# Last pair's scatters in portions, its tile list earlier, row loads bound to later additions

## The chip, the core and the metric

The kernel runs on 1 core of a Trainium2 chip. The metric is the time of one execution in device microseconds, a median of three runs. The engines are PE (TensorE), ACT (ScalarE), DVE (VectorE), POOL (GpSimd) and SP (SyncE, which here only issues transfers). Transfers issued by SP and POOL run on the same 16 DMA engines.

## What is computed

16 sequences of 512 tokens of width 128 go through two blocks. Cut to what matters (`_L0_attn_ref` is a Mamba-2 layer: input projection, convolution, scan, gated norm, output projection):

```python
h = _layernorm(x, axis=-1) * (1 + ca) + sa
x = x + ga * _L0_attn_ref(h, ...)
h = _layernorm(x, axis=-1) * (1 + cb) + sb
x = x + gb * _L0_ffn_ref(h, ...)
# _L0_ffn_ref: mixture of 8 experts, the two best of each token
gout = xt @ Wg.T
topv, topi = jax.lax.top_k(gout, K)
w = jax.nn.softmax(topv, axis=-1)
h = jax.nn.silu(g) * v          # g, v: two projections to 256 by the expert
eo = jnp.einsum('etf,ehf->eth', h, W3) + b3[:, None, :]
out = jnp.einsum('eth,te->th', eo, comb)
```

## The kernel before

The sequences are worked on in 8 pairs (`NP`), 1024 tokens each. For each pair the first block runs in chunks of 128 tokens; its result `x` is stored to `out` in HBM (`store_x1`). Then the router picks two experts for each token, and POOL *scatters* the tokens: 16 indirect transfers of 128 rows (`scatter(p, q)`, L419, two transfers a call, q from 0 to 7) write each token's row (`payload`: 128 values, the gate `gb`, the weight, the token number) to a place in the HBM buffer `rows` that belongs to its expert. q = 4 to 7 write the second choice and need the weights exchanged in `payload` first (`second_weight`, L430, which waits for the landing of the first 8 transfers).

The expert work is cut into 71 *tiles* (`NTILES`) of 256 rows of one expert. DVE writes the *list* of the tiles that have become full, pair by pair (`new_tiles`, L1082): the expert of a tile (`tile_e`) and its first row (`tile_row`). A tile t goes through:

- SP: `load_rows(t)` (L304, transfer at L318) brings 256 rows to `xs[t % 7]`; `load_weights(t)` (L294, transfer at L298) brings one expert's weights, 386 KB, to `wt[t % 4]`.
- PE: `expert_turn` (L1430) transposes the rows, `expert_up(t, 0)` and `(t, 1)` (L1438) make `FG` and `FV`, `expert_down` (L1448) the result in `FX`. ACT copies and takes silu (L652, L643), DVE multiplies (`expert_hidden`, L1120) and weights the result into `xs` (`expert_out`, L1130).
- POOL: `add_out(t)` (L436, transfers at L457) adds the 256 rows to `out` in HBM with two indirect transfers that accumulate.

Two executions of `add_out` that touch the same row must not overlap. The helper `landed(eng, t)` (L255) waits until the addition of tile t, and of all before it of its parity, has landed. `add_out(t)` always waits for `landed(t - 2)`; up to tile 49 it waits for `landed(t - 1)` too, and from tile 50 on only where the list says that the two may clash (`turn_of`, L448).

Tiles 0 to 48 come out of the first seven pairs' lists with a delay of 7 tiles (`LAG`). The last 22 tiles, 49 to 70 (`LAST`), come from the last pair's list. Their rows can be loaded once all 128 scatters have landed and the 8 *pads* have: SP writes 256 rows of zeros behind each expert's last row (`set_pads_of`, L300), called from `load_rows(49)`. `load_rows(t)` waits for the list, for the scatters of its pair, and for `landed(t - 7)`, since `xs` has 7 buffers.

All queues are written out by hand. On each engine a loop over i issues stage i's pieces of pairs i - 1, i, i + 1, i + 2 and of the tiles 8 i - 29 to 8 i - 14, in the written order; every engine works strictly in its order. In stage i = 8 the last pair's scatters are issued, each call between additions of the tiles 40 to 45. SP's order from tile 49 on, `r` for rows and `w` for weights: pads, r49, w49, r50, r51, r52, w50, r53, w51, w52, r54, w53, w54, r55, w55, r56, w56, r57, w57, r58, r59, r60, w58, r61, w59, w60, r62, w61, w62, r63, w63, r64, w64, r65, w65, r66, r67, r68, w66, r69, w67, w68, r70, w69, w70. PE's order in these stages is `expert_up(t, 0)`, `expert_down(t - 1)`, `expert_up(t, 1)`, with `expert_turn` one to three tiles ahead.

Of the kernel before, what the change touches and what calls it, by code (L numbers as in the profile page):

```python
# [30 lines left out]
NP = B // 2  # L31
# [4 lines left out]
PT = 2 * 2 * L // TR  # L36
LAG = E - 1
NTILES = NP * PT + LAG
# [3 lines left out]
DUMP = E * REGION + FIRST  # L42
XR = 3
WR, XSR = 4, 7
DOWN = 2 * FT * P
B12 = DOWN + FT * D
WT = B12 + 2 * FT
# [2 lines left out]
LAST = NTILES - (PT * (NP - 1) - LAG)  # L50
# [10 lines left out]
def program(nc, d):  # L61
    ctx = ExitStack()
    with ctx:  # L63
# [187 lines left out]
        def is_pair(p):  # L251
            return 0 <= p < NP

        def is_tile(t):
            return 0 <= t < NTILES  # L255

        def landed(eng, t):
            if t >= 0:
                eng.wait_ge(added[t % 2], 32 * (t // 2 + 1))
# [6 lines left out]
        @block.sync  # L266
        def _(sp_):
            xv = d["x"].rearrange("b (c p) m -> p b c m", p=P)
            ov = d["out"][0:NTOK, :].rearrange("(b c p) m -> p b c m", p=P, c=C)

            def load_x(p):
                sp_.dma_start(x[:, p % XR, :, :].rearrange("p (k c) m -> p k c m", k=2),
                              xv[:, 2 * p:2 * p + 2, :, :]).then_inc(x_in[p % XR], 16)

            def reload_x(p):
                if p >= XR:
                    sp_.wait_ge(x1_stored, 16 * (p - XR + 1))
                    sp_.wait_ge(xn2_ready, p - XR + 1)
                    load_x(p)

            def store_x1(p):
                sp_.wait_ge(x1_ready, p + 1)
                sp_.dma_start(ov[:, 2 * p:2 * p + 2, :, :],
                              x[:, p % XR, :, :].rearrange("p (k c) m -> p k c m", k=2)).then_inc(x1_stored, 16)

            def load_gates(p):
                wait(sp_, wo_ready, p - 1)
                sp_.dma_start(gate_a[:, p % 2, :, :],
                              d["gates"][2 * p:2 * p + 2, 0:D].partition_broadcast(P)).then_inc(gate_a_in[p % 2], 16)
                wait(sp_, payload_ready, p - 1)  # L290
                sp_.dma_start(gate_b[:, p % 2, :, :],
                              d["gates"][2 * p:2 * p + 2, D:2 * D].partition_broadcast(P)).then_inc(gate_b_in[p % 2], 16)

            def load_weights(t):  # L294
                sp_.wait_ge(seq_ready, pair_of_tile(t) + 1)
                wait(sp_, o_psum, t - WR + 1)
                e = sp_.value_load(tile_e[0:1, t:t + 1], min_val=0, max_val=E - 1)  # L297
                sp_.dma_start(wt[:, t % WR, :], d["wt"][bass.ds(e, 1), :, :].rearrange("o p n -> p (o n)")).then_inc(wt_in[t % WR], 16)  # L298

            def set_pads_of(e):  # L300
                r = sp_.value_load(pad_row[0:1, e:e + 1], min_val=0, max_val=DUMP)
                sp_.dma_start(d["rows"][bass.ds(r, TR), :].rearrange("(c p) m -> p c m", p=P), pad[:, :, :]).then_inc(pads_set, 16)

            def load_rows(t):  # L304
                p = pair_of_tile(t)
                sp_.wait_ge(seq_ready, p + 1)
                if t == 0:
                    sp_.wait_ge(dump_set, 32)
                if t == NTILES - LAST:
                    sp_.wait_ge(pads_ready, 1)  # L310
                    for e in range(E):
                        set_pads_of(e)
                if t >= NTILES - LAST:
                    sp_.wait_ge(pads_set, 16 * E)
                sp_.wait_ge(scattered, 16 * 2 * J * (p + 1))
                landed(sp_, t - XSR)
                r = sp_.value_load(tile_row[0:1, t:t + 1], min_val=0, max_val=DUMP + TR)  # L317
                sp_.dma_start(xs[:, t % XSR, :, :], d["rows"][bass.ds(r, TR), :].rearrange("(c p) m -> p c m", p=P)).then_inc(xs_in[t % XSR], 16)  # L318

            load_x(0)  # L320
            for dst, src in ((table[:, :], "table"), (wmod, "wmod"), (wout, "wout")):
                sp_.dma_start(dst, d[src]).then_inc(consts_in, 16)
            load_x(1)
            sp_.wait_ge(gate_step, 4)
            sp_.dma_start(d["gates"], gate_all).then_inc(gates_out, 16)
            load_x(2)
            sp_.dma_start(b3_rows, d["b3"]).then_inc(b3_in, 16)
            sp_.wait_ge(zero_ready, 1)
            sp_.wait_ge(pad_set, 1)
            sp_.dma_start(d["out"][NTOK:NTOK + 3 * TR, :].rearrange("(c p) m -> p c m", p=P),  # L330
                          zero[:, :].unsqueeze(1).to_broadcast([P, 6, D])).then_inc(dump_set, 16)
            sp_.dma_start(d["rows"][DUMP:DUMP + 2 * TR, :].rearrange("(c p) m -> p c m", p=P), dump_rows).then_inc(dump_set, 16)

            sp_.wait_ge(gates_out, 16)
            for i in range(-1, 13):
                if is_tile(PT * i - 27):
                    load_rows(PT * i - 27)
                if is_tile(PT * i - 29):
                    load_weights(PT * i - 29)
                if is_tile(PT * i - 28):  # L340
                    load_weights(PT * i - 28)
                if is_tile(PT * i - 26):
                    load_rows(PT * i - 26)
                if is_tile(PT * i - 27):
                    load_weights(PT * i - 27)
                if is_tile(PT * i - 26):
                    load_weights(PT * i - 26)
                if is_tile(PT * i - 25):
                    load_rows(PT * i - 25)
                    load_weights(PT * i - 25)  # L350
                if is_pair(i - 1):
                    store_x1(i - 1)
                if is_tile(PT * i - 24):
                    load_rows(PT * i - 24)
                    load_weights(PT * i - 24)
                if is_pair(i + 2):
                    reload_x(i + 2)
                if is_tile(PT * i - 23):
                    load_rows(PT * i - 23)
                    load_weights(PT * i - 23)  # L360
                if is_tile(PT * i - 22):
                    load_rows(PT * i - 22)
                if is_pair(i + 1):
                    load_gates(i + 1)
                if is_tile(PT * i - 21):
                    load_rows(PT * i - 21)
                if is_tile(PT * i - 20):
                    load_rows(PT * i - 20)
                if is_tile(PT * i - 22):
                    load_weights(PT * i - 22)  # L370
            sp_.wait_ge(x1_stored, 16 * NP)
            sp_.wait_ge(dump_set, 32)
            landed(sp_, NTILES - 2)
            landed(sp_, NTILES - 1)

        @block.gpsimd
        def _(pool):
# [58 lines left out]
            def add_out(t):  # L436
# [19 lines left out]
                for c in range(2):  # L456
                    pool.indirect_dma_start(d["out"], bass.IndirectOffsetOnAxis(ap=xs[:, t % XSR, c, PAY - 1:PAY].bitcast(U32), axis=0),  # L457
                                            xs[:, t % XSR, c, 0:D], None, compute_op=ALU.add).then_inc(added[t % 2], 16)

            for i in range(-2, 13):  # L460
                if is_pair(i - 2):
                    scatter(i - 2, 7)
                if is_tile(PT * i - 26):
                    add_out(PT * i - 26)
# [4 lines left out]
                    weight_by_decay(i, 2)  # L469
                if is_tile(PT * i - 25):  # L470
                    add_out(PT * i - 25)
                if is_tile(PT * i - 24):
                    add_out(PT * i - 24)
                if is_pair(i - 1):
# [314 lines left out]
        def _(vec):  # L789
# [340 lines left out]
            def expert_out(t):  # L1130
                vec.wait_ge(o_psum, t + 1)
                for c in range(2):
                    last = nc.vector.scalar_tensor_tensor(out=xs[:, t % XSR, c, 0:D], in0=FX[:, TR + c * D:TR + (c + 1) * D],  # L1133
                                                          scalar=xs[:, t % XSR, c, 2 * D:2 * D + 1], in1=xs[:, t % XSR, c, D:2 * D],
                                                          op0=ALU.mult, op1=ALU.mult)
                last.then_inc(ro_ready, 1)
# [7 lines left out]
            for i in range(-2, 12):  # L1144
# [33 lines left out]
                    softplus_rest(i + 1)  # L1178
                if is_tile(PT * i - 22):
                    expert_out(PT * i - 22)  # L1180
                if is_pair(i + 1):
                    conv_taps(i + 1, 4)
                if is_tile(PT * i - 21):
# [13 lines left out]
                    expert_out(PT * i - 20)  # L1197
                if is_pair(i):
                    mean_square(i)
                if is_pair(i - 1):  # L1200
                    new_tiles(i - 1)
                if is_pair(i):
                    residual(i)
# [38 lines left out]
        def _(pe):  # L1242
# [219 lines left out]
            for i in range(-2, 12):  # L1462
# [121 lines left out]
                if is_pair(i + 1):  # L1584
                    turn_y(i + 1, 0)
                    intra(i + 1, 1)
                if is_tile(PT * i - 15):
                    expert_turn(PT * i - 15)
                if is_pair(i):
                    turn_h2(i)  # L1590
                if is_tile(PT * i - 16):
                    expert_down(PT * i - 16)
                if is_pair(i + 1):
                    new_state(i + 1, 2)
                if is_tile(PT * i - 15):
# [71 lines left out]
```

## Time and profile before

| | us |
|---|---|
| median of 3 runs (823.67 to 825.77) | 825.5 |
| the profiled execution | 832.36 |
| span of its instructions | 830.5 |
| POOL busy, the whole span | 462.0 |
| mean busy share of the DMA engines, 640 to 706 us | 0.67 |
| the same, 729.3 to 822.7 us | 0.72 |
| PE busy, 729.3 to 822.7 us (93.4 us) | 65.9 |
| POOL busy, 729.3 to 822.7 us | 65.4 |

The page comes from one profiled execution; times inside the span count from its start. Busy time leaves out the issue of transfers by the sequencer. In a timeline row the first number is the start, the second the length, and the brackets hold the idle time before it with what ended it; a name as `out<-xs` is what is written and what is read. SPq and POOLq are the sequencers of SP and POOL.

### The profile page before, as it was taken

Reading aid. Unit: us, or ns where it says so; the run is one execution under the profiler, and the core shown is the slowest. Engines: PE = TensorE matmul, PEld = TensorE weight load, DVE = VectorE, ACT = ScalarE, POOL = GpSimd, SP = SyncE. Lnnn points to the kernel's source line nnn. Section 1 sums busy time; section 2 is a strip of 40 time slices with the busy share of each in tenths; the row PEclk is TensorE's granted clock in tenths of the full one; section 3 lists DMA queues with packets and bytes.
Section 4 is the critical chain, followed back from the end, with each engine's and each line's share of the span. In section 5 each row is a group of like instructions: output and inputs, shape, how many; then the busy total and the mean of one; then the engine's idle time right before and its main releaser. Section 6 shows DMA issues by size and latency. Waiting matters only on the chain. (4 is left out here: it accounts for less than half of the span.)

```text
span 830.5 us, 13734 instructions
## 1 busy us (share of the span) xinstructions
PE 680.6 (82%) x3713; PEld 518.9 (62%) x3713; DVE 559.4 (67%) x1640; ACT 516.8 (62%) x1223; POOL 462.0 (56%) x366
## 2 busy tenths in 40 slices
PE   3678899789789999998999999999966952774982
PEld 3246557556567776876787777768755731553662
DVE  2827967988986997898689978987743561231421
ACT  3784795896796899687969977886522310221320
POOL 2003004444453378757775786688687477357775
PEclk9779798999998999999999999999996967897997
DMA  5100001112013465455346444653645774857973
GB/s 186 28 0 1 1 27 32 45 52 71 33 58 102 119 168 129 105 155 125 92 105 174 107 97 103 204 104 90 180 107 120 200 204 95 202 123 149 191 169 28
DMA packets 81275, 88.86 MB, mean 107 GB/s; under 512 B 7360, under 2 KB 67696, under 8 KB 81200
## 3 DMA queue, kind: packets, MB, share of 16 engines
q1 hardware_dynamic: 54528, 61.37, 25.6%
q0 software_dynamic: 26672, 26.62, 18.0%
q8 instruction: 31, 0.51, 0.3%
q14 instruction: 44, 0.36, 0.2%
HBM read 54.50 MB, written 33.46 MB: 106 GB/s over the span
## 5 line engine op out<-in xcount | busy, mean ns | idle before, releaser
L457 POOL DMA_INDIRECT out<-xs x142 | 226.8, 1597 | 116.9 <-issue 53.2
L427 POOL DMA_INDIRECT rows<-payload,pos x128 | 131.6, 1028 | 68.2 <-issue 30.2
L880 DVE SCALAR_TENSOR_TENSOR xbc<-T,table,xbc 128x511 f32<-128x511 f32 (+2 forms) x192 | 141.9, 746 | 7.7 <-ACT xbc L599 3.1
L1133 DVE SCALAR_TENSOR_TENSOR xs<-FX,xs 128x128 f32<-128x128 f32 x142 | 43.1, 345 | 122.6 <-PE FX L1457 104.7
L1457 PE MATMUL FX<-wt,hid 128*128 128x128 f32 x568 | 87.8, 301 | 17.2 <-DVE hid L1125 17.2
L655 ACT ACTIVATE xt<-FX 128x256 f32<-128x256 f32 x71 | 27.0, 380 | 110.1 <-PE FX L1434 96.0
L1457 PEld LDWEIGHTS FX<-wt,hid 128*128 128x128 f32 x568 | 73.7, 203 | 26.6 <-DVE hid L1125 17.9
L648 ACT ACTIVATE sg<-FG,wt 128x256 f32<-128x256 f32 x142 | 59.3, 471 | 47.0 <-PE FG L1444 38.4
L1444 PE MATMUL FG<-xt,wt 128*128 128x256 f32 x284 | 77.6, 397 | 12.1 <-DMA wt<-in_wt 8.1
L1287 PE MATMUL T<-h,win 128*128 128x512 f32 x128 | 76.7, 698 | 12.4 <-DVE xbc L880 10.6
L1444 PE MATMUL FV<-xt,wt 128*128 128x256 f32 x284 | 78.2, 400 | 0.0
L630 ACT ACTIVATE mda<-table,da 128x128 f32<-128x128 f32 x256 | 77.7, 397 | 0.0
L1125 DVE SCALAR_TENSOR_TENSOR hid<-FV,wt,sg 128x256 f32<-128x256 f32 x142 | 62.0, 479 | 22.5 <-issue 13.3
L599 ACT ACTIVATE xbc<-T,table 128x512 f32<-128x512 f32 x64 | 49.5, 773 | 40.3 <-PE T L1287 35.8
L385 POOL TENSOR_TENSOR rstd<-var,table 128x8 f32<-128x8 f32 x16 | 26.6, 1663 | 78.4 <-DVE var L826 63.9
L1346 PEld LDWEIGHTS YA<-xdt,decay 128*128 128x128 f32 x512 | 66.9, 207 | 2.8 <-issue 1.7
L1346 PE MATMUL YA<-xdt,decay 128*128 128x64 f32 x512 | 66.6, 288 | 1.0 <-issue 1.0
L1444 PEld LDWEIGHTS FG<-xt,wt 128*128 128x128 f32 x284 | 52.4, 200 | 20.3 <-DMA wt<-in_wt 9.7
L406 POOL TENSOR_TENSOR xdt<-tok,dt 128x512 f32<-128x512 f32 x32 | 34.8, 1088 | 51.5 <-ACT tok L566 51.3
L527 ACT ACTIVATE xn<-x,shift,rstd 128x128 f32<-128x128 f32 x128 | 50.9, 484 | 17.5 <-DVE shift L844 16.4
L1444 PEld LDWEIGHTS FV<-xt,wt 128*128 128x128 f32 x284 | 52.4, 201 | 8.5 <-issue 3.8
L1434 PE MATMUL FX<-table,xs 128*128 128x128 f32 x142 | 29.3, 290 | 31.8 <-DMA xs<-rows 27.8
(207 smaller groups left out, 1343.5 us busy)
## 6 DMA issues: line engine op xcount, KB each, us to landing
wt<-in_wt SPq DMA_DIRECT2D x71, 386.0 KB
xs<-rows SPq DMA_DIRECT2D x71, 258.0 KB
x<-in_x SPq DMA_DIRECT2D x8, 512.0 KB, 4.3
out<-x SPq DMA_DIRECT2D x8, 512.0 KB
out<-xs POOLq DMA_INDIRECT x142
rows<-pad SPq DMA_DIRECT2D x8, 258.0 KB
rows<-payload,pos POOLq DMA_INDIRECT x128
gate_a<-gates SPq DMA_DIRECT2D x8, 128.0 KB, 4.3
```

Source lines behind the costliest of these rows:

```text
L427: pool.indirect_dma_start(d["rows"], bass.IndirectOffsetOnAxis(ap=pos[:, k, n:n + 1], axis=0), payload[:, n, :], None).then_inc(scattered, 16)
L457: pool.indirect_dma_start(d["out"], bass.IndirectOffsetOnAxis(ap=xs[:, t % XSR, c, PAY - 1:PAY].bitcast(U32), axis=0), xs[:, t % XSR, c, 0 ...
L527: last = nc.scalar.activation(dst[:, j, :], src[:, j, :], ACT.Identity, bias=shift[:, j:j + 1], scale=rstd[:, j:j + 1])
L599: nc.scalar.activation(xbc[:, t, k, :], T[:, k, :], ACT.Identity, bias=conv_b[:, t:t + 1], scale=conv_w[:, t * KC + KC - 1:t * KC + KC]).t ...
L630: last = nc.scalar.activation(mda[:, c, n, :], upto, ACT.Copy, scale=da[:, c * J + n:c * J + n + 1])
L648: last = nc.scalar.activation(sg[:, t % 2, f * TR:(f + 1) * TR], FG[:, f * TR:(f + 1) * TR], ACT.Silu, bias=wt[:, t % WR, B12 + f:B12 + f ...
L880: last = nc.vector.scalar_tensor_tensor(out=xbc[:, t, k, tap:L], in0=T[:, k, 0:L - tap], scalar=w, in1=xbc[:, t, k, tap:L], op0=ALU.mult, ...
L1125: last = nc.vector.scalar_tensor_tensor(out=hid[:, t % 2, f, :], in0=FV[:, f * TR:(f + 1) * TR], scalar=wt[:, t % WR, B12 + FT + f:B12 + F ...
L1287: nc.tensor.matmul(T[:, k, :], win[:, o:o + P], h[:, k * L:(k + 1) * L], start=True, stop=True).then_inc(in_psum, 1)
L1346: last = nc.tensor.matmul(YA[:, o:o + HD], decay[:, c, k, hh, :], xdt[:, c % 2, k, hh * HD:(hh + 1) * HD], start=True, stop=True)
L1444: last = nc.tensor.matmul((FG, FV)[v][:, f * TR:(f + 1) * TR], wt[:, t % WR, w:w + P], xt[:, t % 2, :], start=True, stop=True)
L1457: last = nc.tensor.matmul(FX[:, TR + c * D:TR + (c + 1) * D], hid[:, t % 2, f, c * P:(c + 1) * P], wt[:, t % WR, DOWN + f * D:DOWN + (f + ...
```

## The change

Five edits, all about the last pair and the tiles from 41 on.

1. POOL: in stage 8, the last pair's eight calls of `scatter` are issued in four portions of two calls, ahead of the additions of tiles 40, 41, 42 and 43 (`last_scatters`). The additions of 44 to 49 then follow without a scatter between them.
2. DVE: the last pair's `new_tiles` comes behind `expert_out(42)`, where it came behind `expert_out(44)`.
3. SP: `load_rows(t)` waits for `landed(t - 5)` from tile 41 on, where it waited for `landed(t - 7)`.
4. SP: the weights of tiles 49, 50 and 51 are loaded behind the pads, ahead of the rows of tile 49 (`AHEAD`); the loop's other loads go through `load_weights_of`, which leaves these three out. The wait for the list stands behind the pads and these weights in `load_rows(49)`.
5. PE: `expert_turn(49)` comes behind `expert_down(48)`, where it came ahead of it.

```diff
+AHEAD = 3
...
+            def load_weights_of(t):
+                if not 0 <= t - (NTILES - LAST) < AHEAD:
+                    load_weights(t)
...
             def load_rows(t):
                 p = pair_of_tile(t)
-                sp_.wait_ge(seq_ready, p + 1)
                 if t == 0:
                     sp_.wait_ge(dump_set, 32)
                 if t == NTILES - LAST:
                     sp_.wait_ge(pads_ready, 1)
                     for e in range(E):
                         set_pads_of(e)
+                    for n in range(AHEAD):
+                        load_weights(t + n)
+                sp_.wait_ge(seq_ready, p + 1)
                 if t >= NTILES - LAST:
                     sp_.wait_ge(pads_set, 16 * E)
                 sp_.wait_ge(scattered, 16 * 2 * J * (p + 1))
-                landed(sp_, t - XSR)
+                landed(sp_, t - (XSR if t < NTILES - LAST - PT else XSR - 2))
...
+            def last_scatters(p):
+                t = PT * (p + 1) - 24
+                for n in range(4):
+                    if n == 2:
+                        second_weight(p)
+                    scatter(p, 2 * n)
+                    scatter(p, 2 * n + 1)
+                    add_out(t + n)
+                add_out(t + 4)
+                add_out(t + 5)
+
             for i in range(-2, 13):
-                if is_pair(i - 2):
+                if 0 <= i - 2 < NP - 1:
                     scatter(i - 2, 7)
...
                     add_out(PT * i - 25)
+                if i == NP:
+                    last_scatters(i - 1)
+                    continue
                 if is_tile(PT * i - 24):
...
                     expert_out(PT * i - 22)
+                if i == NP:
+                    new_tiles(i - 1)
                 if is_pair(i + 1):
                     conv_taps(i + 1, 4)
...
-                if is_pair(i - 1):
+                if 0 <= i - 1 < NP - 1:
                     new_tiles(i - 1)
...
-                if is_tile(PT * i - 15):
+                if is_tile(PT * i - 15) and PT * i - 15 != NTILES - LAST:
                     expert_turn(PT * i - 15)
                 if is_pair(i):
                     turn_h2(i)
                 if is_tile(PT * i - 16):
                     expert_down(PT * i - 16)
+                if PT * i - 15 == NTILES - LAST:
+                    expert_turn(PT * i - 15)
```

POOL's queue from the addition ahead of the last pair's calls `scatter(7, 2)` and `scatter(7, 3)` on (L427 in the kernel before and L434 in the changed one is `scatter`, L457 and L464 `add_out`, two transfers a tile; the first row is tile 41 before and tile 40 now), before:

```order
L457 DMA out<-xs 8960x128 x2
L427 DMA rows<-payload,pos 148224x258 x4
L457 DMA out<-xs 8960x128 x2
L432 COPY payload<-wtop 128x8
L427 DMA rows<-payload,pos 148224x258 x2
L457 DMA out<-xs 8960x128 x2
L427 DMA rows<-payload,pos 148224x258 x2
L457 DMA out<-xs 8960x128 x2
L427 DMA rows<-payload,pos 148224x258 x2
L457 DMA out<-xs 8960x128 x2
L427 DMA rows<-payload,pos 148224x258 x2
L457 DMA out<-xs 8960x128 x8
```

and in the changed kernel:

```order
L464 DMA out<-xs 8960x128 x2
L434 DMA rows<-payload,pos 148224x258 x4
L464 DMA out<-xs 8960x128 x2
L439 COPY payload<-wtop 128x8
L434 DMA rows<-payload,pos 148224x258 x4
L464 DMA out<-xs 8960x128 x2
L434 DMA rows<-payload,pos 148224x258 x4
L464 DMA out<-xs 8960x128 x14
```

Four portions of four transfers stand where pairs of transfers alternated with additions, and seven additions (43 to 49, 14 transfers) follow in a row, where the row had four (46 to 49).

SP's queue from the last of the 8 pads on (only its transfers; `rows<-pad` is the pad, `xs<-rows` a `load_rows`, `wt<-in_wt` a `load_weights`), before:

```order
L302 DMA rows<-pad 128x2x258
...
L318 DMA xs<-rows 128x2x258
...
L298 DMA wt<-in_wt 128x772
...
L318 DMA xs<-rows 128x2x258
...
L318 DMA xs<-rows 128x2x258
...
L318 DMA xs<-rows 128x2x258
...
L298 DMA wt<-in_wt 128x772
```

and in the changed kernel:

```order
L307 DMA rows<-pad 128x2x258
...
L299 DMA wt<-in_wt 128x772
...
L299 DMA wt<-in_wt 128x772
...
L299 DMA wt<-in_wt 128x772
...
L325 DMA xs<-rows 128x2x258
...
L325 DMA xs<-rows 128x2x258
...
L325 DMA xs<-rows 128x2x258
...
L325 DMA xs<-rows 128x2x258
```

Three weight loads stand ahead of the rows of tile 49; nothing else changes its place on SP. What changes is what the row loads wait for.

DVE's queue up to the first instruction of the last pair's list, `pad_from`, before (from `expert_hidden(41)` on):

```order
L1125 SCALAR_TENSOR_TENSOR hid<-FV,wt,sg 128x256 x2
L1133 SCALAR_TENSOR_TENSOR xs<-FX,xs 128x128 x2
L1125 SCALAR_TENSOR_TENSOR hid<-FV,wt,sg 128x256 x2
L1133 SCALAR_TENSOR_TENSOR xs<-FX,xs 128x128 x2
L1125 SCALAR_TENSOR_TENSOR hid<-FV,wt,sg 128x256 x2
L1133 SCALAR_TENSOR_TENSOR xs<-FX,xs 128x128 x2
L1125 SCALAR_TENSOR_TENSOR hid<-FV,wt,sg 128x256 x2
L1133 SCALAR_TENSOR_TENSOR xs<-FX,xs 128x128 x2
L1089 TENSOR_TENSOR pad_from<-cum,table 128x8
```

and in the changed kernel:

```order
L1146 SCALAR_TENSOR_TENSOR hid<-FV,wt,sg 128x256 x2
L1154 SCALAR_TENSOR_TENSOR xs<-FX,xs 128x128 x2
L1146 SCALAR_TENSOR_TENSOR hid<-FV,wt,sg 128x256 x2
L1154 SCALAR_TENSOR_TENSOR xs<-FX,xs 128x128 x2
L1110 TENSOR_TENSOR pad_from<-cum,table 128x8
```

The list has two tiles less ahead of it; `expert_hidden` and `expert_out` of 43 and 44 come behind it.

## Rows read from the trace of the kernel before

**Rows 1.** The page, section 5: line engine op out<-in xcount | busy, mean ns | idle before.

```profile
L457 POOL DMA_INDIRECT out<-xs x142 | 226.8, 1597 | 116.9 <-issue 53.2
```

**Rows 2.** Timeline of POOL: start us, us, instruction [idle before <-releaser].

```profile
680.13 1.01 POOL L427 DMA_INDIRECT rows<-payload,pos  x1 [0.81 <-POOL payload L432]
...
684.65 1.58 POOL L457 DMA_INDIRECT out<-xs  x1 [0.30 <-issue]
...
691.97 1.60 POOL L457 DMA_INDIRECT out<-xs  x1 [3.12 <-issue]
...
703.44 0.99 POOL L427 DMA_INDIRECT rows<-payload,pos  x1 [0.30 <-issue]
704.73 1.60 POOL L457 DMA_INDIRECT out<-xs  x1 [0.30 <-issue]
...
712.77 1.55 POOL L457 DMA_INDIRECT out<-xs  x1 [4.56 <-issue]
...
720.89 1.55 POOL L457 DMA_INDIRECT out<-xs  x1 [4.70 <-issue]
...
729.33 1.55 POOL L457 DMA_INDIRECT out<-xs  x1 [5.03 <-issue]
...
822.66 1.56 POOL L457 DMA_INDIRECT out<-xs  x1 [0.30 <-issue]
```

**Rows 3.** Waits of SP's queue, 700 to 830 us: total, times, longest.

```profile
SPq L259 <- DMA out<-xs: 52.7, 11, 19.2
```

**Rows 4.** Timeline of SP, the same columns: transfers it issues.

```profile
673.79 0.39 SPq L318 DMA_DIRECT2D xs<-rows  x1
...
677.64 9.03 SPq L302 DMA_DIRECT2D rows<-pad  x8
706.94 0.39 SPq L318 DMA_DIRECT2D xs<-rows  x1
...
709.49 2.90 SPq L318 DMA_DIRECT2D xs<-rows  x3
...
749.16 6.97 SPq L318 DMA_DIRECT2D xs<-rows  x3
...
782.60 7.00 SPq L318 DMA_DIRECT2D xs<-rows  x3
790.53 0.24 SPq L298 DMA_DIRECT2D wt<-in_wt  x1
```

**Rows 5.** Timeline of DVE around the last pair's list, and the result of tile 49.

```profile
653.59 0.17 DVE L1072 CAST pos<-posf 128x16 uint32<-128x16 f32 x1
...
666.87 0.16 DVE L1089 TENSOR_TENSOR pad_from<-cum,table 128x8 f32<-128x8 f32 x1
...
678.87 0.18 DVE L1117 SCALAR_TENSOR_TENSOR turn_of<-need,table 128x21 int32<-128x21 f32 x1
...
682.03 0.61 DVE L1133 SCALAR_TENSOR_TENSOR xs<-FX,xs 128x128 f32<-128x128 f32 x2 [2.17 <-issue]
...
719.66 0.61 DVE L1133 SCALAR_TENSOR_TENSOR xs<-FX,xs 128x128 f32<-128x128 f32 x2 [3.31 <-PE FX L1457]
```

**Rows 6.** Chain that ended last, in order of time: start us, us, what.

```profile
751.66 3.30 DMA out<-xs
...
756.96 4.15 DMA wt<-in_wt
...
761.15 2.07 PE FG L1444 x4
...
766.90 0.26 POOL out L457
...
814.74 3.36 DMA out<-xs
```

**Rows 7.** Timelines of PE and DVE, 790 to 802 us.

```profile
795.03 1.20 PE L1444 MATMUL FG<-xt,wt 128*128 128x256 f32 x4 [1.69 <-DMA wt<-in_wt]
...
798.60 0.61 DVE L1133 SCALAR_TENSOR_TENSOR xs<-FX,xs 128x128 f32<-128x128 f32 x2 [5.48 <-PE FX L1457]
```

More of the change, by code:

```diff
@@ L338, in _ @@
                 if is_tile(PT * i - 29):
-                    load_weights(PT * i - 29)
+                    load_weights_of(PT * i - 29)
                 if is_tile(PT * i - 28):
-                    load_weights(PT * i - 28)
+                    load_weights_of(PT * i - 28)
                 if is_tile(PT * i - 26):
@@ L344, in _ @@
                 if is_tile(PT * i - 27):
-                    load_weights(PT * i - 27)
+                    load_weights_of(PT * i - 27)
                 if is_tile(PT * i - 26):
-                    load_weights(PT * i - 26)
+                    load_weights_of(PT * i - 26)
                 if is_tile(PT * i - 25):
                     load_rows(PT * i - 25)
-                    load_weights(PT * i - 25)
+                    load_weights_of(PT * i - 25)
                 if is_pair(i - 1):
@@ L354, in _ @@
                     load_rows(PT * i - 24)
-                    load_weights(PT * i - 24)
+                    load_weights_of(PT * i - 24)
                 if is_pair(i + 2):
@@ L359, in _ @@
                     load_rows(PT * i - 23)
-                    load_weights(PT * i - 23)
+                    load_weights_of(PT * i - 23)
                 if is_tile(PT * i - 22):
@@ L369, in _ @@
                 if is_tile(PT * i - 22):
-                    load_weights(PT * i - 22)
+                    load_weights_of(PT * i - 22)
             sp_.wait_ge(x1_stored, 16 * NP)
```

## The prediction

> **What bounds the kernel now.** The page's costliest group is POOL's transfers [rows 1]: 142 that add to `out`, 1.6 us each. With the 0.30 between them a tile costs POOL two pitches of 1.86, 3.72 us, and a scatter 1.29 (0.99 and 0.30, [rows 2]). The chain that ended last runs through the additions, so POOL's timeline is read next [rows 2, 6]. Three stretches show there. Up to the last scatter at 703.44, scatters and additions alternate and POOL is nearly full. The additions of tiles 46 to 49 start at 704.73, 712.77, 720.89 and 729.33: periods of 8.0 to 8.4, since up to tile 49 each waits until the one before it has landed. From 49 (729.33) to 70 (822.66) 21 tiles take 93.3 us, 4.4 each against POOL's own 3.72. SP in turn mostly waits for landed additions [rows 3]: 52.7 us of the last 130. That is the wait that edit 3 makes stricter.
>
> Two durations carry the sum. **A landing**, counted from the start of a tile's second transfer: light, 3.3 to 3.4 (751.66 and 814.74, [rows 6]); beside other loads, 6.2 to 6.6 (tile 46's second transfer 1.86 behind 704.73 until 712.77, likewise 47 and 48, [rows 2]), 7.3 beside the pads (684.65 to 691.97). **A gate**: SP takes its queue in order, so the weights of 58 go out behind the rows of 60, which wait for `landed(53)`; and PE does `expert_up(58, 0)` ahead of `expert_down(57)`. So the addition of 57 cannot start before 53 has landed and weights have come. The trace has this as a chain [rows 6]: landing 751.66 to 754.96, weight issue 756.96, 4.15 to land, PE, ACT and DVE, addition at 766.90. From the first transfer of 53 (751.66 less 1.86) that is **17.1 us**. A second case has the weights of 66 issued at 790.53 [rows 4] and the result of 65 ready at 798.60 + 0.61 [rows 7]: 8.7 from weight issue to result, against 9.9 before. In the kernel before a gate spans four to six tiles, which POOL needs 14.9 us or more for: nearly hidden.
>
> **Edit 1, the scatters.** `pos` is ready at 653.8 [rows 5], so the first portion starts at 654.1. 16 scatters (20.6), three additions (11.2) and 0.5 for the copy of the second weight (0.81 idle instead of 0.30, [rows 2]) end at 686.4; the last starts at 685.1. Before, the last started at 703.44 and the rows of 49 went out at 706.94 [rows 4], 3.5 later; now the scatters have landed at 688.6, 18 us earlier. By itself this moves nothing out of POOL, it moves additions behind it.
>
> **Edits 2 and 3 before tile 43.** The addition of 40 starts at 659.3 behind the first portion, its second transfer at 661.2, landed 6.2 later at 667.4. The rows of 45 waited for `landed(38)`, now for `landed(40)`; behind them go the weights of 43, at 2.0 after the landing (754.96 to 756.96, [rows 6]): 669.4, result of 42 8.7 later, 678.1. Then the list, 12.2 (666.87 to 679.05, [rows 5]), to 690.3, and the result of 43 3.6 behind it (679.05 to 682.64, the same rows): 693.9. The addition of 43 starts at **694** and not at 682.8 (684.65 less 1.86), though POOL is free from 686.4. The list, moved ahead of two tiles, is complete 11 us later than before, since the tile ahead of it comes later.
>
> **From 43 to 49** there are six serial periods and no scatter to fill them. A light one is 1.86 + 3.4 + 0.3 = 5.5, a loaded one 8.2. The rows of 48 now wait for `landed(43)` (they went out at 673.79, [rows 4]), behind them the pads, 9.0 us of issue, then three weights: pads from about 702 to 712 and rows of 49 at about 716, 9 later than before despite the earlier scatters. I take three loaded and three light periods, 41: addition of 49 at 735, **+6**. All light gives 727 (-2), all at 8.4 gives 744 (+15). Before, the result of 49 came at 719.66 + 0.61, 13.3 behind its rows at 706.94 [rows 4, 5]; rows at 716 give 729, which the serial periods hide, and so edit 4's early weights count for nothing. Edit 5 frees the result of 48 early; its addition waits for 47's landing anyway: 0.
>
> **From 49 to 70** every gate is two tiles shorter. With SP's and PE's written order, addition k holds back addition m, 17.1 us from start to start: 49 holds 52 (weights 53), 52 holds 56 (57), 55 holds 57 (58), 56 holds 58 (59), 57 holds 60 (61), 63 holds 65 (66), 65 holds 68 (69). Between them runs 3.72 a tile. Counted from 49: 52 at 17.1, 56 at 34.2, 57 at 28.3 + 17.1 = 45.4, 58 at 51.3, 60 at 62.5, 63 at 73.7, 65 at 90.8, 68 at 107.9, 69 at 114.0 (it waits for 68's landing now as before), 70 at 117.7. Before: 93.3. **+24.4.** The gate is unseen at this length; its ends are 15 (8.7 instead of 9.9 behind the weights, with PE quick: its four `FG` matmuls took 2.07 in the first case, 1.20 in the second [rows 6, 7], 0.9 more) and 20 (a loaded landing), which give 107 and 134: +14 and +40. I take 17.1, the measured chain of the same instructions; the loads are spread thinner, so the light landing in it fits. The last transfer's end is unchanged.
>
> **Sum**: 6 + 24 = +30 on a span of 830.5, 860.5. The profiled execution (832.36) lies 6.9 above the median 825.5, so I carry the difference over: **855.5**.
>
> **The rivals.**
> - *Light landings win* (faster). Behind the scatters SP issued the rows of 49 to 52 and the weights of 49 within 6 us [rows 4], and the additions beside them landed in 6.2 to 6.6, not 3.3. Loads bound to additions cannot bunch. The six periods then give -2. In the tail it decides only where a gate falls under 12 us: at 12 the same sum gives 93.7 for the 21 tiles, at 11 it gives 90, and with no gate binding 85.5 (3.72 a tile and 2.4 more at each of 64, 66 and 69, which wait for the landing before them). So 815 to 820, I put 818. Against it: 1.86, a landing of 3.3, 2.0 of issue and 4.15 of weights are 11.3 before PE has begun. Chance 0.13.
> - *The gates just fit* (no change). SP ran ahead of need, and a gate near 12 gives 93.7 less the 2 of light periods: 824. For it: for 52.7 us of the last 130 SP stood waiting [rows 3] and PE was fed all the same. 0.06.
> - *All landings loaded* (slower still): gate 20 and periods of 8.4 give +40 and +15, 880; with the loads spread, at most some landings are loaded, so I put 875. 0.08.
> - *The earlier scatters do not reach anyone*: part of the forecast, through the pads behind the rows of 48.
>
> The Trainium skill bears on the first rival: "DMA: Bandwidth & Descriptors", section "Latency and other measured facts", puts HBM access latency at 0.2 us on average and 2 us at high load, and calls it the dominant part of a transfer's fixed cost, so lighter load makes each landing cheaper. It speaks for edit 3. The rows agree in direction, 3.3 against 6.2 to 6.6, by more than the page's 1.8. An estimate by the page: all six periods light, which takes 8 us from the sum, 847.5. It says nothing of a load that is issued too late.
>
> **The numbers.** A measurement of this kernel tells from no change what is over 0.3%, 2.5 us. Forecast 0.73, with 837 (gate 15, light periods) to 872 as its own range; rivals as above. Below 820 lies about 0.12, most of the first rival, above 872 about 0.07: range 820 to 872. Faster is the first rival, 0.13, same the second, 0.06, slower the rest, 0.81.
>
> **What would show it.** Scatters end near 686 and the list near 690; addition 43 near 694, 49 near 735; 21 tiles from there take about 118. In the tail SP's rows go out right behind a landing, POOL's idle time falls in blocks ahead of tiles 52, 57, 60, 65 and 68 and is ended by DVE's `xs`, PE waits for `wt`, and landings take 3 to 4 us. It is wrong if POOL still issues every 4 us from 49 on, or if PE never waits for weights there: then a gate costs less than I read from one chain, or the landings were the price all along.

## The result, and the profile after

| | before | changed | |
|---|---|---|---|
| median of 4 runs each, us | 824.59 (823.52 to 825.77) | 865.9 (862.51 to 869.99) | ratio 1.0503 [1.0454, 1.0552] |
| profiled execution, us | 832.36 | 865.94 | +33.6 |
| its span, us | 830.5 | 864.1 | +33.6 |
| up to the first transfer of tile 38 | 640.1 | 636.5 | -3.6 |
| from there to the addition of 49 | 89.2 | 94.2 | +5.0 |
| from 49 to 70 | 93.3 | 125.2 | +31.9 |
| from there to the end | 7.8 | 8.3 | +0.4 |

The changed kernel is 5% slower, 41.3 us by the medians and 33.6 by the profiled executions. The difference of 7.7 comes from the one profiled execution of before, which lay 7.8 above its median, while the changed kernel's lay on its own. The -3.6 up to tile 38 is of the same kind: in the runs below, kernels whose code is the same up to that point reach it at 631.6 to 639.3. The ratios and intervals below leave out two slow executions, one of d1 (852.95 us) and one of g1 (833.53), which lay over 1.5% above the fastest of their kernel.

POOL's timeline of the changed kernel, from the last scatter to the last addition (start us, us, instruction [idle before <-releaser]; of each tile the first transfer):

```profile
682.79 0.97 POOL L434 DMA_INDIRECT rows<-payload,pos  x1 [0.30 <-issue]
689.43 1.61 POOL L464 DMA_INDIRECT out<-xs  x1 [5.67 <-DVE xs L1154]
...
712.90 1.56 POOL L464 DMA_INDIRECT out<-xs  x1 [4.24 <-issue]
...
730.64 1.56 POOL L464 DMA_INDIRECT out<-xs  x1 [2.44 <-issue]
...
737.70 1.56 POOL L464 DMA_INDIRECT out<-xs  x1 [3.64 <-DMA out<-xs]
...
745.38 1.56 POOL L464 DMA_INDIRECT out<-xs  x1 [4.26 <-DMA out<-xs]
...
758.86 1.56 POOL L464 DMA_INDIRECT out<-xs  x1 [2.38 <-DVE xs L1154]
...
763.51 1.56 POOL L464 DMA_INDIRECT out<-xs  x1 [1.23 <-DVE xs L1154]
...
780.95 1.56 POOL L464 DMA_INDIRECT out<-xs  x1 [10.27 <-DVE xs L1154]
...
798.61 1.56 POOL L464 DMA_INDIRECT out<-xs  x1 [6.28 <-DVE xs L1154]
...
811.58 1.56 POOL L464 DMA_INDIRECT out<-xs  x1 [0.30 <-issue]
...
828.83 1.56 POOL L464 DMA_INDIRECT out<-xs  x1 [9.30 <-DVE xs L1154]
...
846.21 1.56 POOL L464 DMA_INDIRECT out<-xs  x1 [6.03 <-DVE xs L1154]
...
855.82 1.56 POOL L464 DMA_INDIRECT out<-xs  x1 [0.30 <-issue]
```

These rows answer to [rows 2]. The additions of 46 to 49 (712.90 to 730.64, three periods) now come every 5.9 to 6.0 us, not every 8.0 to 8.4. From 49 on, those of 50 and 51 still wait for a landing, and the others come in pulses: runs at 3.7 us, and before tiles 57, 60, 65 and 68 (780.95, 798.61, 828.83, 846.21) blocks of 6.0 to 10.3 us in which POOL waits for DVE to finish the result. The window from 49 to 70 (us, then busy time and instructions by engine, granted clock, DMA share, GB/s) says that all that was added is waiting, since POOL is busy for 65.48 us of it, and was for 65.4 before:

```profile
730.60:855.80 125.20, 82.92 (x370) 60.16 (x369) 29.91 (x81) 22.43 (x56) 65.48 (x42) 0.82 0.58 120
```

The chain that ended last shows what DVE was waiting for (start us, us, what):

```profile
765.37 3.53 DMA out<-xs
...
769.70 0.37 SPq L325
...
770.90 4.17 DMA wt<-in_wt
...
775.12 2.07 PE FG L1467 x4
...
777.51 2.00 PE FX L1480 x8
```

This is a gate, link by link as in [rows 6]: the second transfer of 55 lands at 768.90, SP issues the rows of 60 at 769.70 and behind them the weights of 58 at 770.90, they land at 775.07, PE makes `expert_up(58, 0)` and then the result of 57, which POOL adds at 780.95. The chain shows the same group three times more, with weights at 788.43, 818.66 and 836.30.

SP's waits from 700 to 866 us, which answer to [rows 3], and the page's line of `FG`, PE's first work on new weights (line engine op xcount | busy, mean ns | idle before it, what ended it):

```profile
SPq L260 <- DMA out<-xs: 98.6, 21, 19.4
```

```profile
L1467 PE MATMUL FG<-xt,wt 128*128 128x256 f32 x284 | 83.3, 420 | 38.6 <-DMA wt<-in_wt 35.9
```

The same group was, in the kernel before:

```profile
L1444 PE MATMUL FG<-xt,wt 128*128 128x256 f32 x284 | 77.6, 397 | 12.1 <-DMA wt<-in_wt 8.1
```

SP waits 46 us more for landed additions (98.6 against the 52.7 of [rows 3], each up to the end of the program), and PE's idle time that weights end goes from 8.1 to 35.9.

### The profile page after: what moved, and what is told of

Read it like the earlier page. It is cut to its first block and busy times, and to the rows that moved or that the text cites. A ratio compares the mean times of both kernels' runs of the same rounds, so it can differ in the third digit from the quotient of the medians.

```text
span 864.1 us, 13734 instructions
## 1 busy us (share of the span) xinstructions
PE 697.4 (81%) x3713; PEld 527.2 (61%) x3713; DVE 561.6 (65%) x1640; ACT 517.3 (60%) x1223; POOL 463.0 (54%) x366
## 5 line engine op out<-in xcount | busy, mean ns | idle before, releaser
L464 POOL DMA_INDIRECT out<-xs x142 | 227.8, 1605 | 152.8 <-DVE xs L1154 69.5
L434 POOL DMA_INDIRECT rows<-payload,pos x128 | 131.3, 1026 | 71.8 <-DVE pos L1093 33.4
L669 ACT ACTIVATE sg<-FG,wt 128x256 f32<-128x256 f32 x142 | 59.4, 471 | 93.3 <-PE FG L1467 93.2
L1467 PE MATMUL FG<-xt,wt 128*128 128x256 f32 x284 | 83.3, 420 | 38.6 <-DMA wt<-in_wt 35.9
L1480 PE MATMUL FX<-wt,hid 128*128 128x128 f32 x568 | 91.7, 310 | 26.1 <-DVE hid L1146 26.1
L1480 PEld LDWEIGHTS FX<-wt,hid 128*128 128x128 f32 x568 | 77.3, 211 | 35.9 <-DVE hid L1146 26.9
L1310 PE MATMUL T<-h,win 128*128 128x512 f32 x128 | 78.6, 712 | 12.5 <-DVE xbc L901 10.7
L1467 PEld LDWEIGHTS FG<-xt,wt 128*128 128x128 f32 x284 | 54.5, 209 | 49.1 <-DMA wt<-in_wt 38.9
L1467 PE MATMUL FV<-xt,wt 128*128 128x256 f32 x284 | 83.0, 419 | 0.0
L1369 PEld LDWEIGHTS YA<-xdt,decay 128*128 128x128 f32 x512 | 65.1, 203 | 3.5 <-issue 2.4
L1467 PEld LDWEIGHTS FV<-xt,wt 128*128 128x128 f32 x284 | 55.3, 212 | 9.3 <-issue 3.8
```

Of the source, the lines that this page charges most:

```text
L434: pool.indirect_dma_start(d["rows"], bass.IndirectOffsetOnAxis(ap=pos[:, k, n:n + 1], axis=0), payload[:, n, :], None).then_inc(scattered, 16)
L669: last = nc.scalar.activation(sg[:, t % 2, f * TR:(f + 1) * TR], FG[:, f * TR:(f + 1) * TR], ACT.Silu, bias=wt[:, t % WR, B12 + f:B12 + f ...
L1310: nc.tensor.matmul(T[:, k, :], win[:, o:o + P], h[:, k * L:(k + 1) * L], start=True, stop=True).then_inc(in_psum, 1)
L1369: last = nc.tensor.matmul(YA[:, o:o + HD], decay[:, c, k, hh, :], xdt[:, c % 2, k, hh * HD:(hh + 1) * HD], start=True, stop=True)
L1467: last = nc.tensor.matmul((FG, FV)[v][:, f * TR:(f + 1) * TR], wt[:, t % WR, w:w + P], xt[:, t % 2, :], start=True, stop=True)
L1480: last = nc.tensor.matmul(FX[:, TR + c * D:TR + (c + 1) * D], hid[:, t % 2, f, c * P:(c + 1) * P], wt[:, t % WR, DOWN + f * D:DOWN + (f + ...
```

## The experiments

**Theory**: edit 3 is the whole loss. A row load waits for a later addition, and the weights behind it in SP's queue belong to an earlier tile, so addition k holds back an addition two to four behind it for 17 us. **Rivals**: the scatters and the list made the loss (edits 1 and 2); it comes from row loads that are late themselves, not from the weights; the bunching of transfers is what costs, and spacing them would pay if the weights were not behind them. Of each kernel the table gives the median with that of the kernel before on the same chip, the ratio, and two stretches of its profiled execution by POOL's timeline: the addition of 38 to that of 49, and 49 to 70. Rows with the same number of before were measured on one chip, together with it.

| kernel | edit | us (before) | ratio [95%] | 38 to 49 | 49 to 70 |
|---|---|---|---|---|---|
| before | | | | 89.2 | 93.3 |
| changed | all five | 865.9 (824.59) | 1.0503 [1.0454, 1.0552] | 94.2 | 125.2 |
| a1 | changed, edit 3 undone | 831.88 (827.82) | 1.0048 [1.0024, 1.0072] | 89.4 | 96.4 |
| b1 | before, edit 3 alone | 859.94 (827.82) | 1.0388 [1.0346, 1.0429] | 90.7 | 123.4 |
| c1 | changed, weights behind own rows | 846.47 (827.82) | 1.0217 [1.0175, 1.0260] | 94.5 | 105.9 |
| d1 | changed, edit 3 for 41 to 48 only | 839.72 (827.82) | 1.0125 [1.0072, 1.0178] | 101.3 | 94.4 |
| e2 | before, edit 1 alone | 828.17 (824.18) | 1.0046 [1.0021, 1.0071] | 89.2 | 94.7 |
| f1 | before, edit 3 for tile 60 only | 831.58 (824.18) | 1.0096 [1.0066, 1.0126] | 86.6 | 100.8 |
| g1 | a mixture, below | 824.65 (824.18) | 0.9993 [0.9965, 1.0021] | 86.9 | 97.8 |
| h1 | before, weights behind own rows | 819.90 (824.18) | 0.9951 [0.9920, 0.9982] | 85.7 | 92.6 |
| i1 | before, edits 4 and 5 | 825.63 (823.97) | 1.0001 [0.9971, 1.0031] | 87.2 | 94.8 |
| k1 | before, edit 2 alone | 825.18 (823.97) | 1.0020 [0.9992, 1.0048] | 87.4 | 93.9 |
| j1 | h1, edit 3 for 51 to 54 | 823.25 (823.97) | 0.9987 [0.9959, 1.0015] | 86.0 | 95.4 |

### a1: edit 3 undone

```diff
-                landed(sp_, t - (XSR if t < NTILES - LAST - PT else XSR - 2))
+                landed(sp_, t - XSR)
```

> The changed kernel with edit 3 undone: row loads wait for landed(t - 7) again, edits 1, 2, 4 and 5 stay. Gate theory (weights queued behind row loads that wait for an addition too near): the 21 tiles from 49 to 70 go back from 125 to about 93 us, the blocks ahead of 57, 60, 65 and 68 vanish, and the list starts about 10 us earlier. Six serial periods from 43 on start near 686 but are loaded (8.2 each): tile 49 near 732. Sum +3 against the kernel before: 828, between 820 and 834. Rival 'serial additions' (edits 1 and 2 are what costs, since no scatter fills the landings): most of the 41 us stays, 850 or more. Rival 'landings': without the spacing the landings get longer and the time goes above 866.

The other four edits cost 0.5% together. The tail, 49 to 70, takes 96.4 us, and the waits of 6 to 10 us are gone from POOL's timeline; from 52 on, the addition of 57 has the longest period left, 7.6. Edit 3, on top of the others, is thus worth 4.5%, some 37 us. The list starts at 657.41 here and at 673.15 with edit 3, with the same code on DVE.

### b1: edit 3 alone

```diff
-                landed(sp_, t - XSR)
+                landed(sp_, t - (XSR if t < NTILES - LAST - PT else XSR - 2))
```

> The kernel before with edit 3 alone: row loads from tile 41 on wait for landed(t - 5). Gate theory: the start of tile 49 hardly moves (727 to 733), the 21 tiles behind it take about 120 to 125 us as in the changed kernel; +28, 853, between 845 and 860. Rival 'serial additions': edit 3 costs little by itself, under 10 us. Rival 'landings': faster than before.

Alone it costs 32 us and makes a tail (49 to 70) of 123.4 us. POOL's timeline of b1 has the same waits, ahead of the same four tiles, 57, 60, 65 and 68:

```profile
775.20 1.55 POOL L457 DMA_INDIRECT out<-xs  x1 [9.68 <-DVE xs L1133]
...
792.86 1.55 POOL L457 DMA_INDIRECT out<-xs  x1 [6.33 <-DVE xs L1133]
...
823.40 1.55 POOL L457 DMA_INDIRECT out<-xs  x1 [10.34 <-DVE xs L1133]
...
840.65 1.55 POOL L457 DMA_INDIRECT out<-xs  x1 [6.12 <-DVE xs L1133]
```

The four places follow from SP's written order alone; the scatters and the list have no part in them. 32 us of edit 3's 37 are there without the other edits.

### f1: one gate by itself

```diff
-                landed(sp_, t - XSR)
+                landed(sp_, t - (XSR - 2 if t == 60 else XSR))
```

> The kernel before with one wait changed: the rows of tile 60 alone wait for landed(55) instead of landed(53). Gate theory: the addition of 57 starts 17.4 us behind that of 55 instead of 9.4, so 57's period is about 13 us instead of 4.6, no other period grows, and up to 2 us come back behind it because the additions then land lightly: +6 to +8, 0.7 to 1.0%. Rival 'many small delays' (the stricter wait costs a little at every tile by late rows, not at a few weights): no change that can be measured, since one tile in 22 is touched.

One row load waits for two more additions, and the kernel is 7.4 us slower. SP's timeline holds the rows of 58, 59 and 60 in its first row, 14.77 us long, and the weights of 58 behind them; the chain has the same landing, the same weights and PE (start us, us, what):

```profile
739.06 14.77 SPq L318 DMA_DIRECT2D xs<-rows  x3
754.65 0.35 SPq L298 DMA_DIRECT2D wt<-in_wt  x1
```

```profile
749.31 3.34 DMA out<-xs
...
754.65 3.94 DMA wt<-in_wt
758.63 2.08 PE FG L1444 x4
...
764.47 0.26 POOL out L457
```

From the first transfer of 55 (747.45) to that of 57 (764.47) are 17.0 us. The addition of 57 comes 13.3 behind that of 56, against 4.6 before, and POOL, which needs most of the time that is left, doesn't make it up again: the tail is 7.5 longer.

### c1: the weights taken from behind the gate

```diff
+            def early_or_not(t):
+                if t < 52:
+                    load_weights_of(t)
+
+            def load_tile(t):
+                load_rows(t)
+                if t >= 52:
+                    load_weights(t)
```

The loop calls `load_tile` for `load_rows` and `early_or_not` for `load_weights_of`: each tile's weights are issued right behind its own rows, and `landed(t - 5)` stays.

> The changed kernel, landed(t - 5) kept, but on SP the weights of every tile from 52 on go right behind the rows of the same tile, so that no weights wait behind the rows of a later tile. Gate theory: an addition now holds back the one 4 tiles on by weights (17.3 us for 4 tiles, 4.3 a tile) and the one 3 tiles on by rows (about 12.5, 4.2 a tile): 21 tiles in about 95 us instead of 125, time about 836, between 830 and 845. Rival 'the distance to the landing is what counts, whatever the order on SP': the tail stays at 115 us or more and the time above 855.

The waits for weights fall as expected: PE's `FG` idles 14.2 us for them over the whole program, not 35.9. But the tail is 105.9 us, some ten more than expected, and the kernel lies above the 830 to 845 that I had put. Its chain shows why: without the weights, the rows themselves are the gate.

```profile
748.53 3.97 DMA out<-xs
...
753.30 2.85 DMA xs<-rows
...
759.92 0.26 POOL out L473
...
761.78 5.39 DMA out<-xs
...
767.96 2.83 DMA xs<-rows
...
776.32 0.27 POOL out L473
```

The rows of t + 5 wait for addition t, and for five tiles of eight, 54 and 57 among them, PE's written order turns the rows of t + 5 ahead of the result of t + 3. There addition t holds addition t + 3: 51 to 54 takes 746.67 to 759.92, 13.3 us, then 54 to 57 takes 759.92 to 776.32, 16.4, where three additions take POOL 11.2. I had put this second gate at 12.5, from light landings only; in the second pass the landing of 5.39, the four `FG` of 1.29 that stand ahead of the result, and PE's `FX` of 2.00 us for 1.09 make the rest. Weights in the wrong place were 19 of the 29 us between the changed kernel's tail and a1's 96.4; the other 9.5 is what waiting five tiles back still costs. Against h1 below, which has c1's order in the tail and waits seven tiles back, it is 13.3 (105.9 against 92.6).

### d1: edit 3 ahead of tile 49 only

```diff
-                landed(sp_, t - (XSR if t < NTILES - LAST - PT else XSR - 2))
+                landed(sp_, t - (XSR - 2 if NTILES - LAST - PT <= t < NTILES - LAST else XSR))
```

> The changed kernel with landed(t - 5) for tiles 41 to 48 only and landed(t - 7) again from 49 on. Gate theory: the tail takes about 93 us, tile 49 starts near 731 as in the changed kernel since the late list and the pads behind the rows of 48 stay: +4, 829, between 823 and 838. If it comes out at 850 or more, the price of edit 3 lies ahead of tile 49 and not in the tail.

The tail is back at 94.4, so the part from 49 on is what made it long. The part ahead of 49 costs some 7 us against a1 (1.0125 against 1.0048), which put the kernel above the 823 to 838 that I had expected. It stands in 38 to 49 (101.3 against 89.4; in the changed kernel 94.2): the period of addition 43 is 15.1 against 9.0, and that of 46, beside the three early weights, 10.4 against 5.9. In the changed kernel it is 14.3, and DVE's timeline there shows the sequence that the prediction gave, result of 42, list, result of 43:

```profile
672.62 0.61 DVE L1154 SCALAR_TENSOR_TENSOR xs<-FX,xs 128x128 f32<-128x128 f32 x2 [9.20 <-PE FX L1480]
673.15 0.16 DVE L1110 TENSOR_TENSOR pad_from<-cum,table 128x8 f32<-128x8 f32 x1
...
684.86 0.18 DVE L1138 SCALAR_TENSOR_TENSOR turn_of<-need,table 128x21 int32<-128x21 f32 x1
...
688.02 0.61 DVE L1154 SCALAR_TENSOR_TENSOR xs<-FX,xs 128x128 f32<-128x128 f32 x2 [2.17 <-PE FX L1480]
```

### e2, k1, i1: the other edits one by one

e2 makes edit 1 alone, k1 edit 2 alone, i1 edits 4 and 5 alone, each as in the diff ahead of the prediction.

> The kernel before with edit 1 alone: the last pair's scatters in four portions ahead of the additions 40 to 43, seven additions in a row behind them. My theory: the last scatter starts near 683, 20 us earlier, but the six additions from 43 on wait for landings one by one (6 to 8 us each beside pads and row loads), tile 49 starts 0 to 5 us later than before, the tail keeps about 94 us: between -1 and +5 us. Rival 'the scatters were what held the last 22 tiles': tile 49 starts 10 us or more earlier, time under 818.

> The kernel before with edit 2 alone (the last pair's list behind the result of 42 instead of 44). My theory: the additions of 43 to 45 find their results later by up to 12 us of list, but POOL reaches 43 late enough (results of 43 near 676 against an addition at 683 before): 0, between -2 and +3 us. Rival 'an earlier list lets the tail start sooner': tile 49 earlier by 2 us or more.

> The kernel before with edits 4 and 5 alone (weights of 49 to 51 ahead of the rows of 49, PE's turn of 49 behind its down of 48). My theory: 0, between -2 and +3 us: tile 49's addition waits for the landing of 48, not for weights or PE; the three weights, which now go out right behind the pads, may lengthen the landings of 43 and 44. Rival 'early weights start the tail sooner': -3 us or more.

The portions of scatters cost 0.46%, 4 us. In e2 the last of them starts 45.7 us behind the addition of 38, in before 63.4, and these 17.6 us buy nothing. The list alone and the early weights with the later `expert_turn(49)` can't be told from no change. Edit 3 costs 32 us alone and 37 on top of the others. Where these 5 stand is not tested by a kernel of its own; the period of addition 43, 7.1 in b1 and 14.3 in the changed kernel, suggests that edit 3 delays the list once the list comes behind tile 42.

### h1: the better order of SP's queue, by itself

The edit is c1's on the kernel before, with `t < 49` and `t >= 49`, and `landed(t - 7)` kept.

> The kernel before, landed(t - 7) kept, with the weights of every tile from 49 on right behind the rows of the same tile on SP. Gate theory: the two gates left in the kernel before (at 57 and 65) open, the blocks of weight waits on PE go, 21 tiles take 88 to 92 us instead of 93.3: -1 to -5 us, 822. Rival 'crowding': row loads and weights alternating keep DMA engines as busy, the waits for landings two tiles back stay and nothing changes.

This is faster than both kernels, if only by 0.5%: 0.9951 [0.9920, 0.9982], 4.3 us by the medians. SP's timeline shows pairs of rows and weights at POOL's pace, with no block:

```profile
743.03 0.37 SPq L318 DMA_DIRECT2D xs<-rows  x1
744.23 0.35 SPq L298 DMA_DIRECT2D wt<-in_wt  x1
746.76 0.37 SPq L318 DMA_DIRECT2D xs<-rows  x1
747.97 0.35 SPq L298 DMA_DIRECT2D wt<-in_wt  x1
```

The page's line of `FG` has no wait for weights left, in the whole program:

```profile
L1453 PE MATMUL FG<-xt,wt 128*128 128x256 f32 x284 | 76.5, 393 | 2.2 <-issue 2.1
```

The tail takes 92.6, against 93.3 before and 93.9 to 94.8 in i1, k1 and e2, which share before's order of loads from tile 52 on. That is 1 or 2 of the 4 us. Where the others come from I could not locate: profiled executions of one stretch differ by as much.

### g1 and j1: spacing the landings on a good order

g1 is before with edits 4 and 5, the weights behind their rows from 52 on, and `landed(t - 5)` for the rows of 50 to 54 only; j1 is h1 with it for 51 to 54:

```diff
-                landed(sp_, t - XSR)
+                landed(sp_, t - (XSR - 2 if 1 < t - (NTILES - LAST) < 6 else XSR))
```

> A version meant to beat both: the kernel before (its scatters and its list in their old places) with edits 4 and 5, weights of tiles from 52 on right behind their rows, landed(t - 5) for the rows of 50 to 54 only, so that the landings of 46 to 49 are light, and landed(t - 7) elsewhere. Theory: periods of 47, 48 and 49 fall from 8.2 to about 5.9 each (-7), the tail to about 90 (-3): -10, 816, between 811 and 823. Rival 'landings are not made light by spacing': no gain in 47 to 49, time 822 to 826.

> The faster version h1 (weights right behind the rows from 49 on) with landed(t - 5) for the rows of 51 to 54 only and landed(t - 7) elsewhere. Theory: the periods of 47 to 49 fall from 24.0 to about 19 us together, as in g1_best, while tiles 43 and 44 keep their periods since no early weights go out; the tail stays at 93 to 95: -3 us against h1, 817 beside 824 of the kernel before, between 814 and 821. Rival: what the light landings gain comes back in the tail as gates at 53 and 54: no better than h1.

The profiled execution of g1 lay 9 us above its median, so its stretches are only a rough guide. Both show the lighter landings they were made for (periods of 6.9, 5.8 and 6.9 for 47 to 49 in g1), but both miss the 816 and 817 us that I had expected: neither can be told from before, and h1 can. In j1 the additions of 48 and 49 come 6.5 and 6.6 behind those before them (7.6 and 8.2 in h1), as POOL's timeline shows:

```profile
704.48 1.55 POOL L466 DMA_INDIRECT out<-xs  x1 [4.55 <-issue]
...
711.03 1.55 POOL L466 DMA_INDIRECT out<-xs  x1 [3.13 <-issue]
...
717.58 1.55 POOL L466 DMA_INDIRECT out<-xs  x1 [3.14 <-issue]
```

That is 2.8 us gained. The addition of 51 then comes 8.7 behind that of 50, where it was 6.4, since 50 lands beside three pairs of rows and weights that SP issues from 724.38 to 730.83; the tail takes 95.4 instead of 92.6: the 2.8 go back. The transfers held back are the same bytes, and the next additions land beside them. These are single executions: the addition of 44, ahead of anything that j1 changes, came 2.4 us later in j1 than in h1.

## Why the prediction was right, and where it was off

The forecast was 855.5 us, slower, by edit 3; measured are 865.9, slower, and b1 and a1 show edit 3 to be the cause of 32 to 37 of the 41.3 us; e2's 4 us for edit 1 are the next largest part. The mechanism, too, is the one that was forecast: f1 makes one gate by itself. The point times are compared below with 3.6 us taken off the predicted ones, since this execution reached tile 38 that much earlier.

- **Edits 1 to 3 ahead of tile 43**: right. Addition 40 655.7, measured 655.70; list from 674.5, measured 673.15; list complete 686.7, measured 685.04; last scatter 681.5, measured 682.79; addition 43 690.4, measured 689.43.
- **From 43 to 49**: right, 41 us predicted, 41.2 measured. That it came this close is partly luck: three loaded periods (8.2) and three light ones (5.5) were a choice between ends, and the six came as 6.0, 9.8, 7.6, 6.0, 5.9 and 5.9, so two long ones beside the pads and four a little above light. Rows of 49 at 712.4, measured 711.16. That edits 4 and 5 are worth nothing: i1, 1.0001 [0.9971, 1.0031].
- **The gates, 17.1 us each**: right, and this is the sum's largest term. 55 to 57 took 17.44, 57 to 60 17.66, 63 to 65 17.25, 65 to 68 17.38. The prediction's upper end is summed wrongly: by its own rule a gate of 20 us gives a tail of 132, not 134.
- **The tail, 117.7**: 7.5 too small, since other links were left out. Of the 7.5, 4.6 come by tile 55. I had 3.72 a tile wherever no gate binds, though the additions of 50 and 51 still wait for a landing, with periods of 7.1 and 7.7. In before they have periods of 6.7 and 6.3, and I had not read them. The brackets name DVE there, but the result of 50 was ready at 723.67; SP's rows of 56, which wait for 49 to land, went out at 735.94, as the addition of 50 started:

```profile
729.33 1.55 POOL L457 DMA_INDIRECT out<-xs  x1 [5.03 <-issue]
...
736.01 1.55 POOL L457 DMA_INDIRECT out<-xs  x1 [3.26 <-DVE xs L1133]
...
742.35 1.56 POOL L457 DMA_INDIRECT out<-xs  x1 [2.92 <-DVE xs L1133]
```

```profile
735.94 0.38 SPq L318 DMA_DIRECT2D xs<-rows  x1
```

  So 52 comes 18.5 behind 49, not 17.1; the gate from 49 is covered, and no block stands ahead of 52, where one was forecast. Next, the gate that c1 isolates, addition t to t + 3 through the rows alone, was missing from the sum: 51 to 54 took 13.5 us for 11.2, and 55 comes another 0.9 late. So 57 is at 50.3 behind 49, against 45.4. The last big piece is 61, 5.4 behind 60 instead of 3.7: after a gate PE has a whole tile to make before the next result. At 63 the sum is 7.3 short, and little is added after it.
- **The sum**: the forecast is 10.4 us below the result. The span alone was forecast 3.6 too short, 860.5 for 864.1: 7.5 are missing in the tail and 0.4 at the end, less the 3.6 up to tile 38 and 0.7 from there to 49 (94.9 forecast, 94.2 measured). The other 6.9 are the term that I took off because before's profiled execution lay that far above its median; the changed kernel's lay on its own median. Only the 3.6 up to tile 38 came back of it. Some 2.6 stood in 38 to 49: f1, whose code is before's up to tile 49, takes 86.6 there and not 89.2, so that the loss of this stretch is 7.6 rather than the "+6" of the forecast.
- **Rival "light landings win"**: its premise held, its price didn't. Many landings became light (periods of 5.9 and 6.0 ahead of 49; 3.3 to 3.5 us at 765.37 and 782.81), though those of 49, 50 and 53 still took 4.3 to 5.0, and DMA engines were 0.58 busy in the tail instead of 0.72. The rule of the Trainium skill ("DMA: Bandwidth & Descriptors", section "Latency and other measured facts"), that access to HBM takes longer under high load, has the trace's agreement in direction. j1 shows what it is worth here without the gates, 2.8 us, given back two tiles later.
- **Rival "the gates just fit"**: refuted by f1. With one gate made two tiles shorter, 57 came 17.0 behind 55 where before took 9.4; a gate of 12 would have made it 2.6 later, not 7.6; SP's long waits [rows 3] were not spare time, because weights stood behind them.
- **Rival "all landings loaded"**: refuted by the same landings.
- **"The earlier scatters do not reach anyone"**: e2 agrees, with edit 1 costing 4 us and not nothing.

## What to carry to other kernels

When a wait in an in-order queue of loads is made stricter, the price is not the load that waits but what stands behind it: list for each wait the pair "release k holds result m", price one pass through it from the trace, and compare with what the bottleneck engine needs for m - k items. Then order the queue so that nothing for an earlier item stands behind a load for a later one; here that alone, with the old wait kept, gave 0.5%. Read every period of the stretch before calling it free of waits, and where a term is a difference to one profiled execution, allow for that execution's own deviation.

## What was unexpected in the hardware

- **A gate's length varies little**: 16.8 to 17.7 us in ten cases of four kernels (before, changed, b1, f1), though the DMA engines' mean load differed (0.72 and 0.58 in the tails of before and changed). The longest case is a1's from 53 to 57, 18.8 us, where the weights took 4.83 us to land.
- **TensorE's clock falls inside the gate, and takes part of it.** The `windows` view of the changed kernel around the gate of 57 (us, busy time and instructions by engine, granted clock, DMA share, GB/s):

```profile
768.70:770.80 2.10, 0.00 (x0) 0.00 (x0) 0.00 (x0) 0.38 (x1) 1.68 (x2) 1.00 0.36 36
770.80:773.00 2.20, 0.00 (x0) 0.00 (x0) 0.00 (x0) 0.00 (x0) 0.00 (x0) 0.58 0.96 182
...
775.10:777.20 2.10, 2.08 (x5) 1.26 (x5) 0.00 (x0) 0.00 (x0) 0.00 (x0) 0.50 0.86 172
...
783.00:785.00 2.00, 2.00 (x15) 1.62 (x13) 0.91 (x3) 0.34 (x2) 1.37 (x1) 1.00 0.42 35
```

  PE has no instruction from 768.7 to 775.1. The granted clock is at 1.00 (2.4 GHz) at first, drops while PE stands idle, and is at 0.50 (1.2 GHz) when the weights come. The four `FG` matmuls then take 2.07 us and the eight of `FX` 2.00; at full clock the chain has 1.10 and 1.09 for them (799.46 and 801.54). A gate that stops PE thus costs 1.9 us more than its transfers say. The prediction's 17.1 held this, since its `FG` also took 2.07 us [rows 6], at a granted clock of 0.50 in before's trace; the prediction saw the duration but not the clock behind it. A sum from the full-clock durations would have come out short by it at each gate.
- **A landing depends on what shares the DMA engines, over more than a factor of two**: 3.27 us at 782.81 in the changed kernel, 5.39 at 761.78 in c1, and up to 7.3 beside the pads [rows 2]. In j1 spreading the loads moved that time (2.8 us) rather than removing it.
